# First attention of a Flamingo block: transposes of the probabilities cut into two halves of 64 tokens

## The reference

```python
kv_input = jnp.concatenate([layernorm(ctx), layernorm(latents)], axis=1)   # 1178 keys
q, (k, v) = latents_n @ Wq + bq, split(kv_input @ Wkv + bkv)
attn = softmax((q * DH ** -0.5) @ k.T)                 # per head: 1024 x 1178
out = (attn @ v) @ Wo + bo
x = x + tanh(g_xattn[0]) * out
```

## Time and profile before

| what | value |
|---|---|
| time, median of 3 runs | 3241.86 us (3241.77 to 3242.06) |
| profiled execution, its own time | 3246.32 us |
| profiled execution, span of the records | 3244.4 us |
| mean granted TensorE clock | 0.987 of full speed |
| TensorE busy over the span | 3080.4 us (95%) |
| stretch of the 256 steps | about 60 to 1605 us |
| transposes of the probabilities, L751 | 2560 instructions of 128 x 128 |

### The profile page before, as it was taken

The page is one execution under the profiler, slowest core; times in us unless marked ns, Lnnn a source line. Parts: engine busy times, 40 slices in busy tenths (PEclk is TensorE's granted clock), DMA queues, the critical chain, the costliest instruction groups (busy, mean ns, idle before and its releaser), DMA issues. The chain is left out here.

```text
span 3244.4 us, 63785 instructions
## 1 busy us (share of the span) xinstructions
PE 3080.4 (95%) x20804; PEld 2862.1 (88%) x20804; DVE 2460.4 (76%) x4871; ACT 1656.7 (51%) x3147; POOL 778.3 (24%) x1386
## 2 busy tenths in 40 slices
PE   5999999999999999999899999999999989999688
PEld 4999999999999999999888888999999878888576
DVE  6777777777677777878776777878787766667797
ACT  3655555555555555555544422222222256666687
POOL 3232222233222232222111121111111123432220
PEclk9999999999999999999999999999999999999899
DMA  3000000000000000000010124233343300000000
GB/s 102 11 14 11 13 15 12 11 14 9 15 13 12 13 11 13 14 8 6 32 30 5 38 88 114 91 112 99 94 117 94 91 27 1 0 0 0 1 20 33
DMA packets 117390, 114.07 MB, mean 35 GB/s; under 512 B 39630, under 2 KB 83078, under 8 KB 117126
## 3 DMA queue, kind: packets, MB, share of 16 engines
q1 hardware_dynamic: 117126, 110.75, 11.7%
HBM read 105.46 MB, written 5.24 MB: 34 GB/s over the span
## 5 line engine op out<-in xcount | busy, mean ns | idle before, releaser
L454 ACT ACTIVATE x_pth<-x_ps 128x512 fp32r<-128x512 f32 (+1 forms) x768 | 376.0, 528 | 254.7 <-PE x_ps L751 252.2
L1107 ACT ACTIVATE moe_sil<-moe_ps,all_b 128x512 f32<-128x512 f32 x256 | 176.1, 688 | 543.7 <-PE moe_ps L1291 539.4
L555 DVE TENSOR_TENSOR x_ptl<-x_ps,x_pth 128x512 fp32r<-128x512 f32 (+1 forms) x768 | 402.9, 552 | 31.1 <-ACT x_pth L454 19.2
L474 ACT ACTIVATE all_buf<-all_buf,x_nmx 128x1178 f32<-128x1178 f32 x256 | 327.6, 1280 | 129.6 <-DVE all_buf L590 129.4
L751 PE MATMUL x_ps<-ident,all_buf 128*128 128x128 f32 x2560 | 365.7, 274 | 6.1 <-DVE x_ptl L555 6.0
L590 DVE TENSOR_SCALAR_CACHE_REDUCE all_buf<-x_ps 128x1182 f32<-128x1182 f32 x256 | 354.5, 1385 | 22.1 <-PE x_ps L762 13.1
L1316 PE MATMUL moe_ps<-moe_w2z,moe_gh 128*128 128x256 f32 (+1 forms) x1280 | 368.8, 288 | 2.1 <-DVE moe_gl L1241 2.0
L1316 PE MATMUL moe_ps<-moe_w2z,moe_gl 128*128 128x256 f32 x1280 | 362.2, 283 | 0.0
L1316 PE MATMUL moe_ps<-moe_w2l,moe_gh 128*128 128x256 f32 x1280 | 362.0, 283 | 0.0
L777 PE MATMUL x_ps<-x_pth,x_vh 128*128 128x256 f32 x1152 | 346.3, 301 | 0.0
L777 PE MATMUL x_ps<-x_ptl,x_vh 128*128 128x256 f32 x1152 | 325.3, 282 | 0.0
(11 more groups left out here) (382 smaller groups left out, 8128.9 us busy)
## 6 DMA issues: line engine op xcount, KB each, us to landing
moe_gate<-moe_cw_rows SPq DMA_DIRECT2D x512, 128.0 KB, 2.9
all_buf<-in_L_ffn_w_dram SPq DMA_DIRECT2D x16, 512.0 KB, 5.6
xres<-in_x_dram SPq DMA_DIRECT2D x4, 1024.0 KB, 9.5
x_rawk<-in_L_xattn_Wkv_dram SPq DMA_DIRECT2D x32, 128.0 KB, 2.2
x_rawq<-in_L_xattn_Wq_dram SPq DMA_DIRECT2D x32, 128.0 KB, 2.2
x_rawv<-in_L_xattn_Wkv_dram SPq DMA_DIRECT2D x16, 256.0 KB, 2.8
x_rawo<-in_L_xattn_Wo_dram SPq DMA_DIRECT2D x32, 128.0 KB, 2.0
out_dram<-xres SPq DMA_DIRECT2D x8, 512.0 KB, 2.9
```

The source lines that it names most:

```text
L454: act.activation(turn_dst(pth, x, lo, hi), turn_src(x, g), ACT.Copy).then_inc(hi_done, 1)
L474: act.activation(p[:, w % 4, DUP:DUP + R_KV], p[:, w % 4, DUP:DUP + R_KV], ACT.Exp, bias=nmx[:, w % 2:w % 2 + 1], scale=-1.0, accum_out=su ...
L555: last = dve.tensor_tensor(turn_dst(ptl, x, lo, mid), turn_src(x, g)[:, 0:mid - lo, :], turn_dst(pth, x, lo, mid).bitcast(F32), ALU.subtract)
L1107: act.activation(dst[:, q % 2, :], ps[:, HID + q % 2, :], ACT.Silu, bias=bias).then_inc(silu_done, 1)
```

## The change

Each block of 128 tokens x 128 keys is no longer transposed by one instruction over 128 partitions, but by two over 64 partitions each: tokens 0 to 63 into bank 3, tokens 64 to 127 into bank 4, each 64 columns wide. Eight blocks (of 64 columns) then fill both banks, so the ten blocks of a tile go in two bursts of eight and two, in place of three of four, four and two. Copy and subtraction keep their number and their sizes: one for each bank of the first burst (128 x 512), and one over both banks for the second (128 x 256). The waits change with it: a burst now writes both banks, so it waits for all subtractions of the burst ahead of it. The bursts keep their places in the step. A semaphore increment (`alone`) stands behind the waits.

```diff
-        READ0, TURN0, LOW0, JLOW0, SPLIT0, ADD0 = 1, 12, 2, 2, 1, 1
+        READ0, TURN0, LOW0, JLOW0, SPLIT0, ADD0 = 1, 8, 2, 2, 1, 1
-        GRP = ((0, 4), (4, 8), (8, R_BLK))
+        GRP = ((0, 8), (8, R_BLK))
+        HALF = P // 2
...
-        def turn_src(x, g):
-            lo, hi = GRP[g]
-            return ps[:, TURN + (x + g) % 2, 0:(hi - lo) * P].rearrange("p (n t) -> p n t", t=P)
-
-        def turn_dst(t, x, lo, hi):
-            return t[:, (x // 2) % 2, lo:hi, (x % 2) * P:(x % 2 + 1) * P]
+        def turn_piece(i):
+            return (GRP[0], slice(i, i + 1)) if i < 2 else (GRP[1], slice(0, 2))
+
+        def turn_src(i, lo, hi):
+            (first, last), halves = turn_piece(i)
+            bank = ps[:, TURN + halves.start:TURN + halves.stop, 0:(last - first) * HALF]
+            return bank.rearrange("p r (n t) -> p r n t", t=HALF)[:, :, lo - first:hi - first, :]
+
+        def turn_dst(t, x, i, lo, hi):
+            blocks = t[:, (x // 2) % 2, lo:hi, (x % 2) * P:(x % 2 + 1) * P]
+            return blocks.rearrange("p n (r t) -> p r n t", t=HALF)[:, turn_piece(i)[1], :, :]
...
-            def high(b, x, g):
-                lo, hi = GRP[g]
-                act.wait_ge(turned, 3 * (STEPS * b + x) + g + 1 + TURN0)
-                act.activation(turn_dst(pth, x, lo, hi), turn_src(x, g), ACT.Copy).then_inc(hi_done, 1)
+            def high(b, x, i):
+                (lo, hi), _ = turn_piece(i)
+                act.wait_ge(turned, 2 * (STEPS * b + x) + i // 2 + 1 + TURN0)
+                act.activation(turn_dst(pth, x, i, lo, hi), turn_src(i, lo, hi), ACT.Copy).then_inc(hi_done, 1)
...
-                if g == 2:
+                if g == 1:
                     pe.wait_ge(tail_set, X + 1)
-                pe.wait_ge(lo_done, 3 * X + g - 1 + LOW0)
+                pe.wait_ge(lo_done, 3 * X + 2 * g + LOW0)
+                pe.sem_inc(alone, 1)
                 for n in range(lo, hi):
-                    last = pe.transpose(ps[:, TURN + (x + g) % 2, (n - lo) * P:(n - lo + 1) * P],
-                                        p[:, x % 4, DUP + n * P:DUP + (n + 1) * P], ident[:, :])
+                    for r in range(2):
+                        rows = slice(r * HALF, (r + 1) * HALF)
+                        last = pe.transpose(ps[:, TURN + r, (n - lo) * HALF:(n - lo + 1) * HALF],
+                                            p[rows, x % 4, DUP + n * P:DUP + (n + 1) * P], ident[rows, rows])
                 last.then_inc(turned, 1)
...
                     turn(b, x, 0)
-                    turn(b, x, 1)
...
-                    turn(b, x, 2)
+                    turn(b, x, 1)
```

More of the change, by code:

```diff
@@ L333, in _ @@
             reload(BATCH - 1, False)
-            sp.wait_ge(turned, 3 * (STEPS * BATCH - 2) + TURN0)
+            sp.wait_ge(turned, 2 * (STEPS * BATCH - 2) + TURN0)
             load_moe_weights(sp, A, S, 0, 0)
             load_moe_weights(sp, A, S, 0, 1)
-            sp.wait_ge(turned, 3 * STEPS * BATCH + TURN0)
+            sp.wait_ge(turned, 2 * STEPS * BATCH + TURN0)
             load_moe_weights(sp, A, S, 0, 2)
@@ L549, in job, with low @@
                 last.then_inc(job_high, 1)
-            def low(b, x, g):
-                lo, hi = GRP[g]
-                dve.wait_ge(hi_done, 3 * (STEPS * b + x) + g + 1)
+            def low(b, x, i):
+                (lo, hi), _ = turn_piece(i)
+                dve.wait_ge(hi_done, 3 * (STEPS * b + x) + i + 1)
                 mid = min(hi, R_FULL)
-                last = dve.tensor_tensor(turn_dst(ptl, x, lo, mid), turn_src(x, g)[:, 0:mid - lo, :], turn_dst(pth, x, lo, mid).bitcast(F32),
+                last = dve.tensor_tensor(turn_dst(ptl, x, i, lo, mid), turn_src(i, lo, mid), turn_dst(pth, x, i, lo, mid).bitcast(F32),
                                          ALU.subtract)
@@ L558, in low @@
                     r = slice(R_SET, 2 * R_SET)
-                    dst = turn_dst(pth, x, mid, hi)[r, :, :]
-                    last = dve.tensor_tensor(dst, turn_src(x, g)[r, mid - lo:hi - lo, :], dst.bitcast(F32), ALU.subtract)
+                    dst = turn_dst(pth, x, i, mid, hi)[r]
+                    last = dve.tensor_tensor(dst, turn_src(i, mid, hi)[r], dst.bitcast(F32), ALU.subtract)
                 last.then_inc(lo_done, 1)
@@ L588, in step @@
                     dve.wait_ge(s_done, W + 1)
-                    dve.wait_ge(turned, 3 * W - 9 + TURN0)
+                    dve.wait_ge(turned, 2 * W - 6 + TURN0)
                     dve.tensor_scalar(p[:, w % 4, 0:3 * SN].rearrange("p (b c) -> p b c", c=SN), scores, -1.0, R_BIG, ALU.mult, ALU.min,
```

## The result

The changed kernel takes 3329.3 us (median of 4, 3325.4 to 3334.1) against 3242.0 us: ratio 1.0262, 95% interval 1.0249 to 1.0275, so 87 us slower. The forecast was 3484 us, with a range of its own of 3435 to 3510; 3324 us was rival B, the full overlap of the two halves, which had been given a chance of 0.20. The profiled execution of the changed kernel has a span of 3327.6 us.

The account below looks back on a forecast made before the run. TensorE, busy 95% of the span, was taken as the bound. Terms of 42 + 169 + 31 = +242 us on the median 3241.9 gave 3484 us; own range 3435 to 3510, 8-in-10 range 3310 to 3510.

Parts of the forecast that it names:

- rival B: Transposes: the two halves of a pair overlap fully, with holes and later wait kept; +82 us, 3324 us, chance 0.20.
- part 1: Half transposes on TensorE: 0.0625 us each without overlap, +42 us; bounds +0.16 and -0.46 us a step.
- Part 2: Going in and out of 64 partitions on TensorE: 0.33 us an excursion, two a step in 256 steps, +169 us.
- Rivals C and D: No holes around the halves: C with full overlap, 3189 us, chance 0.06; D without overlap, 3349 us, chance 0.04.
- Part 3: Last burst's later wait for both subtractions: TensorE stops 0.30 us in 103 of the 256 steps, +31 us.
- Part 4: Items priced at nothing: copies and subtractions keep number and size, and the semaphore increment ahead of each burst adds nothing.
- T1: Account drawn after the result, used for the experiments: 0.32 us per burst of halves, 0.066 us a pair, plus later-wait stops.

Follow-up runs that it names:

- e_same: The changed kernel with both halves of every block read from partitions 0 to 63, none from the other tokens: 3478.8 us.
- e_extra: The changed kernel with one more whole transpose ahead of the fifth block of each first burst, cutting its halves in two: 3431.8 us.
- e_mid: The changed kernel with the second burst put behind the first three value matmuls instead of ahead of them: 3295.2 us.
- e_wh: The changed kernel with whole transposes in the first burst (eight blocks) and halves only in the second (two blocks): 3353.9 us.
- e_hw_early2: The changed kernel with whole transposes in the second burst, into bank 3 alone, waiting only for the first bank's subtraction: 3241.5 us.
- e_ww_early: The changed kernel with whole transposes in both bursts, the second into bank 3 alone, waiting only for the first bank's subtraction: 3259.5 us.
- e_serial: The changed kernel with each burst reordered, all halves of tokens 0 to 63 first, then all of tokens 64 to 127: 3405.7 us.

## Why the prediction was wrong

**The step that failed is part 1, the choice between its two bounds.** The prediction took "no overlap, since the 0.061 between weight loads is the tightest spacing that the trace has and nothing shows two loads at once". All four halves from which that came lay on the same 64 partitions, as the text itself says. The row could not speak for or against halves on different ones, and nearness of form was taken for evidence. The term was +42 us and is -118: ten slots of 0.0625 us in place of ten transposes of 0.109. e_same shows both that the slot was priced rightly (+233 us against the forecast's +242) and that pairing is what the forecast missed.

**Part 2 held.** 0.33 us an excursion was read from two places outside the bursts; the changed kernel has 0.34 and 0.34, and e_extra 0.29. Two in a step make 2 x 0.34 x 256 = 174 us, against 169. This is what makes the change slower. Rivals C and D, which have no holes, are out by these rows and by e_extra. How the prediction divided an excursion was wrong: by the earlier trace rows the way in is 1658.75 - 1658.54 - 0.119 = 0.09 us and the way out 0.24, not 0.14 and 0.20. Only their sum enters the forecast.

The Trainium skill, "TensorEngine Tiling (Array Packing)", Key Properties, names both effects, the drain at a change of mode and tiles that load and multiply in parallel. The traces agree with both: 0.34 us, and two loads in one slot. The prediction believed the first, which rows confirmed, and gave the second only the chance of rival B.

**Part 3 held.** Stops of 0.30 us in 103 steps were forecast at 31 us. The timeline has 0.35, the starts over the whole stage have a median of 0.35 in 104 places behind score matmuls, and e_mid gives 34. In the waits these stops are split: 21.6 us in 75 places for the subtraction, 14.1 us in 33 places as "issue".

**Part 4 held** where it was tried: the increment is worth about 2 us. Copies and subtractions keep their mean lengths (527 against 528 ns, and 552 both times).

With the one term exchanged the sum is -118 + 174 + 34 = +90 us, against 87 measured. By distances between starts in the two traces, the first bursts with their way in and out take 11 us less than before and the second ones 99 us more. So all of the loss is at the burst of two blocks and its stops. The direction came out as forecast only because excursions and stops together outweigh either bound of part 1.

**What stays open:** of the 10 us between T1's and the measured price of halves in the second burst of e_wh, the trace has some 4 at the second bursts and the rest spread over other matmuls of the stage. Holes of excursions and stops overlap, and no kernel here takes the two apart at 10 us. Why a change between 128 and 64 partitions costs 0.34 us, and whether pairing needs the two banks, no run shows.

## What to carry to other kernels

A transpose over 128 partitions cut into two over 64 saved 0.047 us here when its halves lay on different partitions and stood next to each other (they always went to two banks; one bank was not tried); getting in and out of such a burst cost 0.34 us. So, by these two prices, a burst needs more than seven blocks to gain anything: eight are barely worth it (e_hw_early2 is 18 us under e_ww_early, and 4 us under before), two are a loss, and a wait that the new bank layout makes longer can cost as much again. When a trace has the new operation's shape, look at which partitions its rows were on before taking its price; and when one bound of a term moves the result by 160 us, the nearest row is a reason only if it could have shown the other case.

## What the runs showed of the hardware that was not expected

- Two weight loads of 64 partitions x 128 columns start and end together (x2 with 0.14 us, the length of one), and so does a pair of their matmuls, which start 3 to 4 ns apart: 0.0625 us a pair. Four instructions thus pass in 0.0625 us, so the 0.0625 us of a lone half is not a limit on issuing instructions.
- The pairing reaches over distance: with eight halves of one kind ahead of eight of the other, six of the sixteen loads still ran two at a time (e_serial).
- A change between 128 and 64 partitions and back cost 0.29 to 0.34 us with every neighbour that was seen: value, score, projection or expert matmuls, or whole transposes of the same kind (e_extra).
